# Split-f16 gate product, centred output weights and squares on ScalarE in a recurrent block with a mixture of experts

## The chip, the cores and the metric

The kernel runs on one core of one Trainium2 chip. The metric is the device time of one execution in microseconds (us). The engines are PE (TensorE), DVE (VectorE), ACT (ScalarE), POOL (GpSimd) and SP (SyncE, which here only issues DMAs). Each works through its own list of instructions in the order of the program and stops at a semaphore wait until another engine has counted it up.

## The reference

4096 tokens (16 sequences of 256) of 256 values go through two residual layers, each between layer norms. The first is the recurrent one, and it is all that the change touches:

```python
xp = layernorm(x) @ W_in.T
i, f, o, c = split(xp @ W_gate.T + b_gate)       # 4 heads x 64
i, f, o, c = exp(i), sigmoid(f), sigmoid(o), tanh(c)
cell_t = f_t * cell_{t-1} + i_t * c_t
h = o * tanh(cell * rsqrt(mean_64(cell**2) + 1e-6) * rms_w)
x = x + layernorm(h @ W_out.T)
# then x = x + layernorm(experts(layernorm(x))): router, top 4 of 16 experts, gate/up and down products
```

## The kernel before

**Stages.** First the kernel multiplies W_in into W_gate (L485), so that a block needs one gate product with a combined 256 x 1024 weight `WcT`. Then come eight blocks of 512 tokens, in ten software steps (`steps`, s = 0 to 9): step s makes the gates of block s, the cell, hidden state and output product of block s-1, and the second norm, router and routing of block s-2. POOL scatters each routed block to memory (L916, 16 indirect DMAs a block). When all are scattered, 144 tiles of 128 routed rows go through the experts (L624 to L655, L942), and the end adds and normalises (L1310 on). Every instruction's place is written by hand; there is no scheduler.

**A step on PE.** The gate product of a block has eight chunks c of 128 gate columns; each is a matmul of 512 columns for each of the two halves of the contraction (L502), into PSUM bank 2 or 3 in turn. Between them stand: after c=1 `mean_square` (L510), after c=3 the transposing and spreading of the RMS factors (L516, L525) and the transposes of block s-2 (L541), after c=4 the router (L553) and `out_product` (L533, which gives y in PSUM banks 4 and 5), before c=7 the transposes of the next block's x (L493, PSUM banks 0 and 1). In the trace each f32 matmul has two records.

**A step on ACT.** `gate_chunk` applies tanh or exp to each chunk (L723). After c=5 it also halves f (L702) and does the router's exp (L783). Weight work of the expert stage fills places (`weight_work`): squares (L792) and high halves (L804). Before chunk 7's gate `evac_x` copies the next x to `xT` (L702, two copies), once PE is through with chunk 7; behind it stand `norm_y` (L772, four instructions), `row_high` (L702) and, in the next step, `square` of the cell (L757).

**A step on DVE.** `scan` (L1010, L1016) of block s-1; `residual` of block s-2 (L1032, then statistics L1023 to L1028); `row_low` (L1118) and a weight's low half (`low`, L1211); `block_norms` (L1044 to L1055: three Newton turns on all inverse roots at once; PE's L516 waits for them); the router's tails and `slots` (L1157 to L1164, for which L553 and POOL wait); `scale_cell` (L1089), `hidden` (L1094, for which L533 waits); `choose` (L1100 to L1113); `y_stats` (L1023, on y in PSUM) and `y_norm` (L1069 to L1085, an inverse root on 128 x 4 values by Newton). The next step begins with the next `scan`, directly behind.

**At the start** DVE normalises block 0, then waits for the small weights (L989), prepares constants up to `kb_ready` (L998), for which PE's first gate product waits, and goes through the statistics of blocks 1 to 4.

The lines that decide the two orders on ACT and DVE:

```python
                    if c == CHUNKS - 1 and mid:
                        norm_y(s - 1)
...
                if mid:
                    y_stats(s - 1)
                    list(y_norm())
```

## Time and profile before

| what | value |
|---|---|
| median of 3 runs | 798.14 us (797.46 to 798.87) |
| profiled execution, its own time | 802.32 us |
| its span (first to last instruction) | 800.5 us |
| busy PE, DVE, ACT, POOL | 635.2, 537.2, 458.7, 396.1 us |
| recurrent stage (start to the last scatter) | about 0 to 369 us |
| expert tiles | about 372 to 720 us |
| end | to 800.5 us |
| granted PE clock, mean of the execution | 0.859 of 2.4 GHz |

Times in the rows are of that one execution. "x8" is a count of instructions in a row; a time in square brackets is how long the engine was idle before the row, with the engine that released it. A row's time runs from its first start to its last end, and neighbouring instructions overlap by some 0.1 us. The clock column is the share of 2.4 GHz that the chip granted TensorE; it has two levels, 1.2 and 2.4 GHz.

### The profile page before, as it was taken

The page shows a single profiled execution, that of the slowest core. Times are in us where ns is not written, and L with a number is a line of the kernel's source. Part 1 is how long each engine was busy: PE and PEld are TensorE (multiplying, and loading weights), DVE is VectorE, ACT ScalarE, POOL GpSimd, SP SyncE. Part 2 cuts the span into 40 slices and gives each one's busy share as a digit, 9 for nine tenths or more (in the row PEclk, how much of TensorE's full clock was granted, in tenths as well). Part 3 has the DMA queues.
Part 4 walks back from the last instruction along what each step waited for, and adds up shares of the span by engine and source line. Part 5 has one row for each costly group of instructions (what it writes and reads, how often), then busy time and mean ns, then how long its engine had stood idle before and what let it go on. Part 6 is the DMA issues. An engine that isn't in the chain of part 4 may idle for free.

```text
span 800.5 us, 13282 instructions
## 1 busy us (share of the span) xinstructions
PE 635.2 (79%) x3658; PEld 408.9 (51%) x3658; DVE 537.2 (67%) x1570; ACT 458.7 (57%) x933; POOL 396.1 (49%) x300
## 2 busy tenths in 40 slices
PE   5887979598998752302999999999999999997450
PEld 2344636264565541201666666666666666664230
DVE  3637487778878978500777777777777777771892
ACT  2777686547546533101666767767767767762242
POOL 0012214654845737752466666666666656565121
PEclk9979798889989856555999999999999999997555
DMA  7966754799522223253677777776777676645987
GB/s 250 423 238 106 150 92 71 224 318 347 158 86 101 89 72 119 106 207 99 112 114 110 111 113 111 108 114 109 113 113 114 108 114 102 108 58 76 350 149 102
DMA packets 111895, 115.35 MB, mean 144 GB/s; under 512 B 31730, under 2 KB 101506, under 8 KB 110162
## 3 DMA queue, kind: packets, MB, share of 16 engines
q0 software_dynamic: 35456, 50.35, 37.2%
q1 hardware_dynamic: 76370, 64.16, 26.7%
q8 instruction: 34, 0.56, 0.3%
q14 instruction: 35, 0.29, 0.1%
HBM read 55.15 MB, written 59.31 MB: 143 GB/s over the span
## 4 chain that ended last, share of the span: by engine, by line
PE 59%; DVE 12%; DMA 8%; POOL 7%; ACT 6%; issue 5%; SPq 2%; POOLq 0%; ACTq 0%; DVEq 0%
PE PS L633 8%; PE PS L634 8%; PE PS L635 8%; PE PS L502 7%; POOL routed L916 6%; PE PS L624 4%; PE PS L653 4%; PE PS L641 4%; PE PS L654 4%; PE PS L655 4%; PE PS L525 2%; PE PS L533 2%; DMA W<-w_dn 2%; DMA W<-neg_mem 1%; DVE small L1325 1%
## 5 line engine op out<-in xcount | busy, mean ns | idle before, releaser
L942 POOL DMA_INDIRECT sums<-arena x144 | 223.2, 1550 | 143.8 <-ACT arena L702 71.5
L916 POOL DMA_INDIRECT routed<-arena,small x128 | 142.7, 1115 | 90.6 <-DVE small L1162 45.3
L1303 DVE TENSOR_SCALAR arena<-PS,small 128x256 f32<-128x256 f32 x144 | 78.3, 544 | 126.7 <-ACT arena L875 124.7
L702 ACT ACTIVATE arena<-PS 128x512 f16<-128x512 f16 (+1 forms) x180 | 105.1, 589 | 78.7 <-PE PS L624 45.7
L502 PE MATMUL PS<-arena 128*128 128x512 f32 x256 | 134.0, 668 | 10.7 <-ACT arena L702 10.6
L875 ACT ACTIVATE arena<-PS,small 128x256 f32<-128x256 f32 x144 | 68.1, 473 | 104.1 <-PE PS L635 104.1
L633 PE MATMUL PS<-W,arena 128*128 x288 | 110.2, 382 | 0.0
L634 PE MATMUL PS<-W,arena 128*128 x288 | 110.1, 382 | 0.0
L635 PE MATMUL PS<-W,arena 128*128 x288 | 109.9, 382 | 0.0
L502 PEld LDWEIGHTS PS<-arena 128*128 128x128 f32 x256 | 51.9, 214 | 69.3 <-issue 65.8
L624 PE MATMUL PS<-ident,arena 128*128 128x128 f16 x576 | 56.3, 221 | 36.7 <-DMA arena<-routed 35.9
L624 PEld LDWEIGHTS PS<-ident,arena 128*128 128x128 f16 x576 | 44.4, 99 | 71.6 <-issue 39.7
L653 PE MATMUL PS<-W,arena 128*128 x288 | 78.5, 273 | 2.5 <-DVE arena L1293 2.5
L654 PE MATMUL PS<-W,arena 128*128 x288 | 78.6, 273 | 0.0
L655 PE MATMUL PS<-W,arena 128*128 x288 | 78.5, 273 | 0.0
L927 POOL DMA_DIRECT2D W<-neg_mem x16 | 19.7, 1478 | 114.5 <-ACT W L792 114.5
L723 ACT ACTIVATE arena<-PS,small 128x512 f32<-128x512 f32 x64 | 43.6, 691 | 56.3 <-PE PS L502 56.1
L1305 DVE SCALAR_TENSOR_TENSOR arena<-arena,small 128x256 f32<-128x256 f32 x144 | 69.9, 485 | 5.1
L702 ACT ACTIVATE arena<-PS,arena 128x256 f32<-128x256 f32 x144 | 69.6, 483 | 3.8 <-PE PS L655 3.7
L1293 DVE SCALAR_TENSOR_TENSOR arena<-PS,small,arena 128x256 f16<-128x256 f32 x144 | 68.8, 479 | 1.7 <-ACT arena L702 1.7
L702 ACT ACTIVATE arena<-PS,small 128x256 f16<-128x256 f32 x144 | 68.5, 476 | 0.0
L1304 DVE SCALAR_TENSOR_TENSOR arena<-arena,PS 128x256 f32<-128x256 f32 x144 | 59.2, 411 | 0.0
(164 smaller groups left out, 1023.3 us busy)
## 6 DMA issues: line engine op xcount, KB each, us to landing
arena<-routed SPq DMA_DIRECT2D x144, 128.0 KB
W<-w_gu SPq DMA_DIRECT2D x8, 1024.0 KB, 23.6
W<-neg_mem POOLq DMA_DIRECT2D x16, 512.0 KB, 8.5
sums<-zero SPq DMA_DIRECT2D x2, 4096.0 KB, 26.2
...
```

What stands on the lines that cost most here:

```text
L502: last = mm(PS[:, 2 + c % 2, :], WcT[:, k, c * P:(c + 1) * P], xT[:, k, :], start=(k == 0), stop=(k == KT - 1))
L624: last = nc.tensor.transpose(xT16[:, k * P:(k + 1) * P], xrow[j % UN][:, k * P:(k + 1) * P], ident16[:, :])
L633: mm(acc, xq[j % NX][:, k, :], hi, start=(k == 0), stop=False)
L634: mm(acc, xq[j % NX][:, k, :], lo, start=False, stop=False)
L635: last = mm(acc, xq[j % NX][:, KT + k, :], hi, start=False, stop=(k == KT - 1))
L653: mm(acc, ah[j % 2][:, k, :], hi, start=(k == 0), stop=False)
L654: mm(acc, ah[j % 2][:, k, :], lo, start=False, stop=False)
L655: last = mm(acc, al[j % 2][:, k, :], hi, start=False, stop=(k == KT - 1))
L702: return nc.scalar.activation(o, i, ACT.Copy, **kw)
L916: pool.indirect_dma_start(routed, bass.IndirectOffsetOnAxis(ap=idx, axis=0), rows[b][:, jk // TOPK, :], None).then_inc(rows_sent[lane], 16)
L942: pool.indirect_dma_start(sums[j % SUMS], bass.IndirectOffsetOnAxis(ap=dst[j % MU], axis=0), yb[u], None, compute_op=ALU.add).then_inc(y_s ...
L1303: L.send(v.tensor_scalar(up[j % 2], acc[:, FF:2 * FF], gu_hi, gu_lo, ALU.min, ALU.max))
```

## The change

Four edits, all in the recurrent stage.

- `WcT` and `xT` are held as pairs of f16 arrays, a high half and the remainder, after scaling by powers of two. A gate chunk is then three f16 products for each half of the contraction (high x high, high x low, low x high): six matmuls of 512 columns. The scale of `WcT` comes from its largest magnitude, found at the start.
- ACT's `evac_x` writes x's high half; a new DVE function `x_low` makes the low half, at the end of each DVE step, behind `y_norm`. The weight's halves are made at the start by ACT and DVE.
- The columns of W_out are centred once at the start, so that y has mean zero. Instead of DVE's statistics of y in PSUM, ACT sums its squares (`square_y`, at chunk 6), and DVE's `y_stats` waits for them.
- `norm_y` is gone. `residual` multiplies y in PSUM by its inverse root and adds it to x, in four instructions.

```diff
@@ -185,9 +185,10 @@
             return arena[0:parts, lo:lo + n]
 
 
-        WcT = cut(KT * GATES).rearrange("p (k g) -> p k g", k=KT)
+        WcT = cut(KT * GATES).bitcast(f16).rearrange("p (h k g) -> p h k g", h=2, k=KT)
         xn = cut(BT * DIM).rearrange("p (j d) -> p j d", j=BT)
-        xT = cut(KT * BLK).rearrange("p (k t) -> p k t", k=KT)
+        xT_flat = cut(KT * BLK)
+        xT = xT_flat.bitcast(f16).rearrange("p (h k t) -> p h k t", h=2, k=KT)
         g_i, g_c, g_f = [cut(PART).rearrange("p (k t) -> p k t", k=PAIRS) for _ in range(3)]
         cell = cut(PART).rearrange("p (k t) -> p k t", k=PAIRS)
         stage = at[0]
...
@@ -482,7 +484,7 @@
             for n in range(2):
                 for m in range(KT):
                     for k in range(KT):
-                        last = mm(PS[:, 2 * n + m, :], WiT[:, k, m * P:(m + 1) * P],
+                        last = mm(PS[:, 4 + 2 * n + m, :], WiT[:, k, m * P:(m + 1) * P],
                                   WgT[:, k, n * 512:(n + 1) * 512], start=(k == 0), stop=(k == KT - 1))
                     last.then_inc(wc_mm, 1)
 
...
@@ -496,11 +498,16 @@
             def gates(t, c):
                 if t or c >= 2:
                     pe.wait_ge(gate_act, 8 * t + (c - 1))
+                if c == 0:
+                    pe.wait_ge(xT_ready, KT * (t + 1))
+                    pe.wait_ge(xl_ready, KT * (t + 1))
+                if t == 0 and c % (CHUNKS // 2) == 0:
+                    pe.wait_ge(wc_low, KT * (c // (CHUNKS // 2) + 1))
                 for k in range(KT):
-                    if c == 0:
-                        pe.wait_ge(xT_ready, 2 * t + (k + 1))
-                    last = mm(PS[:, 2 + c % 2, :], WcT[:, k, c * P:(c + 1) * P], xT[:, k, :],
-                              start=(k == 0), stop=(k == KT - 1))
+                    whi, wlo = [WcT[:, h, k, c * P:(c + 1) * P] for h in range(2)]
+                    mm(PS[:, 2 + c % 2, :], whi, xT[:, 0, k, :], start=(k == 0), stop=False)
+                    mm(PS[:, 2 + c % 2, :], whi, xT[:, 1, k, :], start=False, stop=False)
+                    last = mm(PS[:, 2 + c % 2, :], wlo, xT[:, 0, k, :], start=False, stop=(k == KT - 1))
                 last.then_inc(gate_mm, 1)
 
             def mean_square(t):
...
@@ -528,6 +535,8 @@
 
             def out_product(t):
                 pe.wait_ge(h_ready, t + 1)
+                if t == 0:
+                    pe.wait_ge(wr_ready, 4)
                 for j in range(BT):
                     for q in range(PAIRS):
                         last = mm(PS[:, 4 + j // 2, (j % 2) * DIM:(j % 2 + 1) * DIM], hT[:, q, j * P:(j + 1) * P],
...
@@ -596,9 +605,10 @@
                         ranks(s - 2)
 
             pe.wait_ge(s_const, 32)
+            pe.wait_ge(peak_ready, 1)
+            nc.tensor.transpose(PS[:, 2, 0:P], spread, ident).then_inc(peak_mm, 1)
+            transposes_x(0)
             pe.wait_ge(s_w, 16 * 8)
-            pe.wait_ge(wc_copy, 4)
-            transposes_x(0)
             pe.wait_ge(kb_ready, 1)
             steps(step)
 
...
@@ -701,15 +711,10 @@
             def copy(o, i, **kw):
                 return nc.scalar.activation(o, i, ACT.Copy, **kw)
 
-            for n in range(2):
-                for m in range(KT):
-                    act.wait_ge(wc_mm, 2 * n + m + 1)
-                    copy(WcT[:, m, n * 512:(n + 1) * 512], PS[:, 2 * n + m, :]).then_inc(wc_copy, 1)
-
             def evac_x(t):
                 for k in range(KT):
                     act.wait_ge(xT_mm, 2 * t + (k + 1))
-                    copy(xT[:, k, :], PS[:, k, :]).then_inc(xT_ready, 1)
+                    copy(xT[:, 0, k, :], PS[:, k, :], scale=float(2 ** X_BITS)).then_inc(xT_ready, 1)
 
             def gate_chunk(t, c):
                 kind, q = c // 2, c % 2
...
@@ -722,7 +727,7 @@
                 act.wait_ge(gate_mm, 8 * t + (c + 1))
                 nc.scalar.activation((g_c, g_i, g_f, g_o[t % 2])[kind][:, q, :], PS[:, 2 + c % 2, :],
                                      ACT.Exp if kind == 1 else ACT.Tanh, bias=bG[:, c:c + 1],
-                                     scale=1.0 if kind < 2 else 0.5).then_inc(gate_act, 1)
+                                     scale=g_whole if kind < 2 else g_half).then_inc(gate_act, 1)
                 if c == 5:
                     act.wait_ge(gate_act, 8 * t + 6)
                     copy(g_f, g_f, bias=0.5, scale=0.5).then_inc(f_ready, 1)
...
@@ -764,14 +769,14 @@
                 act.wait_ge(cn_ready, t + 1)
                 nc.scalar.activation(cn, cn, ACT.Tanh, scale=rmsw).then_inc(tanh_ready, 1)
 
-            def norm_y(t):
-                act.wait_ge(r2_ready, t + 1)
+            def square_y(t):
+                act.wait_ge(y_mm, t + 1)
                 if t:
                     act.wait_ge(log_mm, t)
                 for j in range(BT):
                     last = nc.scalar.activation(yn[:, j, :], PS[:, 4 + j // 2, (j % 2) * DIM:(j % 2 + 1) * DIM],
-                                                ACT.Identity, bias=mr2[:, j:j + 1], scale=r2[:, j:j + 1])
-                last.then_inc(yn_ready, 1)
+                                                ACT.Square, accum_out=ysq[:, j:j + 1])
+                last.then_inc(ysq_ready, 1)
 
             def evac_x2(t):
                 for k in range(KT):
...
@@ -826,8 +831,8 @@
                         evac_x(s + 1)
                     if new:
                         gate_chunk(s, c)
-                    if c == CHUNKS - 1 and mid:
-                        norm_y(s - 1)
+                    if c == CHUNKS - 2 and mid:
+                        square_y(s - 1)
                     if c == CHUNKS - 1 and old:
                         row_high(s - 2)
                     if c == 1 and on(s, -1):
...
@@ -844,6 +849,10 @@
             act.wait_ge(r1_ready, 1)
             norm_x(0)
             evac_x(0)
+            act.wait_ge(wc_scaled, 1)
+            for n in range(2):
+                for m in range(KT):
+                    copy(WcT[:, 0, m, n * 512:(n + 1) * 512], PS[:, 4 + 2 * n + m, :], scale=wc_scale).then_inc(wc_high, 1)
             act.wait_ge(half_b, 1)
             steps(step)
 
...
@@ -986,6 +995,37 @@
             dve.wait_ge(s_x[0], 16)
             stats_x(0)
             norms_x(0, BT)
+            for i in range(2 * KT):
+                dve.wait_ge(wc_mm, i + 1)
+                last = v.tensor_reduce(wc_peak[:, i:i + 1], PS[:, 4 + i, :], AX, ALU.max, apply_absolute_value=True)
+            L(last)
+            L(v.tensor_reduce(peak, wc_peak, AX, ALU.max))
+            v.tensor_copy(spread, peak.to_broadcast([P, P])).then_inc(peak_ready, 1)
+            dve.wait_ge(peak_mm, 1)
+            L(v.tensor_reduce(peak_all, PS[:, 2, 0:P], AX, ALU.max))
+            L(v.tensor_scalar(expo, peak_all.bitcast(i32), 23, None, ALU.logical_shift_right))
+            L(v.tensor_scalar(expo, expo, EXP_LOW, None, ALU.max))
+
+            def power(o, sign, exponent):
+                return v.tensor_scalar(o.bitcast(i32), expo, sign * 2.0 ** 23, exponent * 2.0 ** 23, ALU.mult, ALU.add)
+
+            power(wc_scale, -1, 268).then_inc(wc_scaled, 1)
+            power(g_whole, 1, -14 - X_BITS)
+            power(g_half, 1, -15 - X_BITS).then_inc(wc_scaled, 1)
+            dve.wait_ge(wc_scaled, 2)
+
+            def x_low(t):
+                for k in range(KT):
+                    dve.wait_ge(xT_ready, KT * t + k + 1)
+                    v.scalar_tensor_tensor(xT[:, 1, k, :], PS[:, k, :], float(2 ** X_BITS), xT[:, 0, k, :],
+                                           ALU.mult, ALU.subtract).then_inc(xl_ready, 1)
+
+            x_low(0)
+            for i in range(2 * KT):
+                n, m = i // KT, i % KT
+                dve.wait_ge(wc_high, i + 1)
+                v.scalar_tensor_tensor(WcT[:, 1, m, n * 512:(n + 1) * 512], PS[:, 4 + i, :], wc_scale,
+                                       WcT[:, 0, m, n * 512:(n + 1) * 512], ALU.mult, ALU.subtract).then_inc(wc_low, 1)
             dve.wait_ge(s_w, 16 * 8)
             v.tensor_scalar(bG[:, 4:8], bG[:, 4:8], 0.5, None, ALU.mult).then_inc(half_b, 1)
             v.tensor_tensor(WrT[:, 0, :], WrT[:, 0, :], r_sub, ALU.subtract).then_inc(wr_ready, 1)
...
@@ -997,6 +1037,10 @@
             v.tensor_copy(ident16[:, :], ident).then_inc(ident16_ready, 1)
             v.tensor_copy(KB[:, :], KBf).then_inc(kb_ready, 1)
             L(v.tensor_copy(dest, K[:, C_DEST:C_DEST + BT]))
+            L(v.tensor_reduce(wo_mean, WoT, AX, ALU.add))
+            L(v.tensor_scalar(wo_mean, wo_mean, 1.0 / DIM, None, ALU.mult))
+            for q in range(PAIRS):
+                v.tensor_scalar(WoT[:, q, :], WoT[:, q, :], wo_mean[:, q:q + 1], None, ALU.subtract).then_inc(wr_ready, 1)
             dve.wait_ge(s_x[1], 16)
             stats_x(1)
             norms_x(BT, 2 * BT)
...
@@ -1028,8 +1072,11 @@
                 L(v.tensor_scalar(nv[:, 0:BT], mv[:, :, 1], eps, None, ALU.add))
 
             def residual(t):
-                dve.wait_ge(yn_ready, t + 1)
-                L(v.tensor_tensor(block_x(t), block_x(t), yn, ALU.add))
+                for j in range(BT):
+                    last = v.scalar_tensor_tensor(block_x(t)[:, j, :], PS[:, 4 + j // 2, (j % 2) * DIM:(j % 2 + 1) * DIM],
+                                                  r2[:, j:j + 1], block_x(t)[:, j, :], ALU.mult, ALU.add)
+                last.then_inc(res_done, 1)
+                dve.wait_ge(res_done, t + 1)
                 stats(lambda j: block_x(t)[:, j, :], mv3, LN_EPS)
 
             def block_norms(t, mid, old, ahead):
...
@@ -1060,10 +1107,10 @@
 
             def y_stats(t):
 
-                dve.wait_ge(y_mm, t + 1)
-                stats(lambda j: PS[:, 4 + j // 2, (j % 2) * DIM:(j % 2 + 1) * DIM], mv2, 4 * LN_EPS)
-
-            def y_norm(done=r2_ready):
+                dve.wait_ge(ysq_ready, t + 1)
+                L(v.tensor_scalar(nv[:, 0:BT], ysq, 1.0 / DIM, 4 * LN_EPS, ALU.mult, ALU.add))
+
+            def y_norm():
 
                 a, b, y, x = na[:, 0:BT], nb_[:, 0:BT], ny[:, 0:BT], nv[:, 0:BT]
                 n = L.send(v.tensor_scalar(a.bitcast(i32), x.bitcast(i32), 1, None, ALU.logical_shift_right))
...
@@ -1082,7 +1129,6 @@
                     n = L.send(v.scalar_tensor_tensor(r2 if turn == 2 else y, b, 1.5, y, ALU.add, ALU.mult))
                 yield
                 L.wait(n)
-                v.scalar_tensor_tensor(mr2, mv2[:, :, 0], -1.0, r2, ALU.mult, ALU.mult).then_inc(done, 1)
 
             def scale_cell(t):
                 dve.wait_ge(rb_mm, t + 1)
...
@@ -1257,6 +1300,8 @@
                     list(y_norm())
                 if s == 3:
                     peak_row(0)
+                if on(s, -1):
+                    x_low(s + 1)
                 if s == 8:
                     low()
                 if s == NBLK + 1:
```

ACT, around the output product of step 5 (L723, now L728, are the gates' activations; L804, now L809, a weight's high half; L702 x2, now L712 x2, are `evac_x`; L772 `norm_y`; L777 `square_y`). Before:

```order
L723 ACTIVATE arena<-PS,small 128x512
L702 ACTIVATE arena<-arena 128x1024
L783 ACTIVATE small<-small 128x16
L723 ACTIVATE arena<-PS,small 128x512
L804 ACTIVATE W<-W,small 128x1024
L702 ACTIVATE arena<-PS 128x512 x2
L723 ACTIVATE arena<-PS,small 128x512
L772 ACTIVATE arena<-PS,small 128x256 x4
L702 ACTIVATE arena<-x_own 128x4x256
L757 ACTIVATE arena<-arena 128x1024
```

The same place in the changed kernel:

```order
L728 ACTIVATE arena<-PS,small 128x512
L712 ACTIVATE arena<-arena 128x1024
L788 ACTIVATE small<-small 128x16
L728 ACTIVATE arena<-PS,small 128x512
L777 ACTIVATE arena,small<-PS 128x256 x4
L809 ACTIVATE W<-W,small 128x1024
L712 ACTIVATE arena<-PS 128x512 x2
L728 ACTIVATE arena<-PS,small 128x512
L712 ACTIVATE arena<-x_own 128x4x256
L762 ACTIVATE arena<-arena 128x1024
```

The four instructions on y have moved ahead of the weight's high half and of `evac_x`, and none stands between `evac_x` and the cell's square.

DVE, end of step 4 and beginning of step 5, before (L1023 to L1028 are `y_stats`, L1069 to L1085 `y_norm`, of which the Newton turns are left out; then `scan` and `residual`):

```order
L1023 BN_STATS small<-PS 128x6 x4
L1026 BN_AGGR small<-small 128x2 x4
L1028 TENSOR_SCALAR small<-small 128x4
L1069 TENSOR_SCALAR small<-small 128x4
...
L1085 SCALAR_TENSOR_TENSOR small<-small 128x4
L1010 TENSOR_TENSOR arena<-arena 128x1024
L1016 SCALAR_TENSOR_TENSOR arena<-arena 128x256 x4
L1032 TENSOR_TENSOR X<-X,arena 128x1024
```

The same place in the changed kernel (L1111 `y_stats`, L1116 on `y_norm`, L1020 `x_low`, L1054 and L1060 `scan`, L1076 `residual`):

```order
L1111 TENSOR_SCALAR small<-small 128x4
L1116 TENSOR_SCALAR small<-small 128x4
...
L1020 SCALAR_TENSOR_TENSOR arena<-PS,arena 128x512 x2
L1054 TENSOR_TENSOR arena<-arena 128x1024
L1060 SCALAR_TENSOR_TENSOR arena<-arena 128x256 x4
L1076 SCALAR_TENSOR_TENSOR X<-PS,small,X 128x256 x4
```

The statistics are one instruction on 128 x 4 values; two instructions of `x_low` stand ahead of the scan, and the residual is four instructions instead of one.

DVE at the start, changed kernel, between block 0's norm and the constants (L1000 to L1010 find the weight's scale, L1020 is `x_low` of block 0, L1027 the weight's low halves; before, L990, now L1030, followed the norm directly):

```order
L991 SCALAR_TENSOR_TENSOR small<-small 128x4
L1000 TENSOR_REDUCE small<-PS 128x1 x4
L1002 TENSOR_REDUCE small<-small 128x1
L1003 COPY prod<-small 128x128
L1005 TENSOR_REDUCE small<-PS 128x1
L1006 TENSOR_SCALAR small<-small 128x1
L1007 TENSOR_SCALAR small<-small 128x1
L1010 TENSOR_SCALAR small<-small 128x1 x3
L1020 SCALAR_TENSOR_TENSOR arena<-PS,arena 128x512 x2
L1027 SCALAR_TENSOR_TENSOR arena<-PS,small,arena 128x512 x4
L1030 TENSOR_SCALAR small<-small 128x4
```

These 15 instructions now stand ahead of the constants (L1038 among them, which frees PE's first gate product) and of the statistics of blocks 1 to 4.

## Rows read from the trace of the kernel before

**Rows 1.** The chain that ended last, 205 to 246 us: shares by line, and one piece.

```profile
by line: PE PS L502 43.5%; PE PS L533 8.7%; ACT arena L772 6.8%; PE PS L510 6.4%; PE PS L525 5.9%; ACT arena L702 5.3%; PE PS L541 4.6%; PE PS L493 4.5%; issue 4.3%; PE PS L553 4.1%; ACT arena L723 3.1%; ACT arena L757 2.3%; ACT small L702 
...
236.90 3.43 PE PS L502 x8
```

**Rows 2.** Timeline of PE: start us, us, instruction, count, idle before it and its releaser.

```profile
94.97 3.70 PE L533 MATMUL PS<-arena 128*128 128x256 f32 x16
...
118.99 0.28 PE L516 MATMUL PS<-K,small 128*16 128x128 f32 x1 [3.17 <-DVE small L965]
...
129.24 3.70 PE L533 MATMUL PS<-arena 128*128 128x256 f32 x16
...
168.22 3.70 PE L533 MATMUL PS<-arena 128*128 128x256 f32 x16
...
192.24 0.28 PE L516 MATMUL PS<-K,small 128*16 128x128 f32 x1 [1.47 <-DVE small L965]
...
200.12 3.70 PE L533 MATMUL PS<-arena 128*128 128x256 f32 x16
...
224.16 0.27 PE L516 MATMUL PS<-K,small 128*16 128x128 f32 x1
...
233.20 3.70 PE L533 MATMUL PS<-arena 128*128 128x256 f32 x16
...
255.58 0.27 PE L516 MATMUL PS<-K,small 128*16 128x128 f32 x1
...
263.10 3.70 PE L533 MATMUL PS<-arena 128*128 128x256 f32 x16
```

**Rows 3.** Timeline of ACT behind an output product.

```profile
176.04 1.14 ACT L804 ACTIVATE W<-W,small 128x1024 f16<-128x1024 f32 x1
178.16 1.09 ACT L702 ACTIVATE arena<-PS 128x512 f32<-128x512 f32 x2 [0.99 <-PE PS L502]
...
179.70 1.94 ACT L772 ACTIVATE arena<-PS,small 128x256 f32<-128x256 f32 x4
```

**Rows 4.** Timeline of DVE in the same stretch, and one row of step 6.

```profile
174.35 0.23 DVE L1028 TENSOR_SCALAR small<-small 128x4 f32<-128x4 f32 x1
...
176.90 1.22 DVE L1010 TENSOR_TENSOR arena<-arena 128x1024 f32<-128x1024 f32 x1
...
181.67 1.23 DVE L1032 TENSOR_TENSOR X<-X,arena 128x1024 f32<-128x1024 f32 x1 [0.97 <-ACT arena L772]
...
222.00 0.17 DVE L1055 SCALAR_TENSOR_TENSOR small<-small 128x4 f32<-128x4 f32 x1
```

**Rows 5.** Timeline of ACT, 31 to 34 us: the squares of a weight slab.

```profile
31.82 1.06 ACT L792 ACTIVATE W<-W 128x1024 bf16<-128x1024 f32 x1 [0.72 <-DMA W<-w_dn]
32.78 0.19 ACT L792 ACTIVATION_READ_ACCUMULATOR W<-W 128x1 f32 x1
```

**Rows 6.** Page, part 5: a VectorE subtraction of halves over 256 columns.

```profile
L1293 DVE SCALAR_TENSOR_TENSOR arena<-PS,small,arena 128x256 f16<-128x256 f32 x144 | 68.8, 479 | 1.7 <-ACT arena L702 1.7
```

**Rows 7.** The same operation over 1024 columns: duration ns min/median/max.

```profile
L1211 DVE SCALAR_TENSOR_TENSOR W<-W,small x24: 1272/1282/1285, 60.6 to 308.7; 128x1024 f16<-128x1024 f32 x24
```

**Rows 8.** The chain at 500 us: one f16 product of 512 columns.

```profile
500.89 0.22 PE PS L633
```

**Rows 9.** Timeline of ACT, DVE and PE at the start.

```profile
16.27 0.60 ACT L702 ACTIVATE arena<-PS 128x512 f32<-128x512 f32 x1 [1.12 <-PE PS L485]
...
17.49 0.27 DVE L998 CAST KB<-W 128x256 bf16<-128x256 f32 x1
...
20.84 1.67 PE L502 MATMUL PS<-arena 128*128 128x512 f32 x2
```

**Rows 10.** Timeline of DVE: its wait for block 6 of x.

```profile
153.25 1.41 DVE L973 BATCH_NORM_STATS2 small<-X 128x6 f32<-128x256 f32 x4 [2.90 <-DMA X<-x]
```

**Rows 11.** Timeline of POOL: first scatter behind its last wait for VectorE.

```profile
295.41 0.97 POOL L916 DMA_INDIRECT routed<-arena,small  x1 [10.59 <-DVE small L1162]
```

**Rows 12.** One stretch: length; PE, PEld, DVE, ACT, POOL busy; clock; DMA share; GB/s.

```profile
116.00:130.00 14.00, 10.66 (x49) 8.10 (x50) 10.25 (x39) 7.44 (x14) 0.22 (x1) 0.76 0.01 1
```

27 lines of the change are left out of this document (13 added, 14 removed).

## The prediction, made before the changed kernel ran

> **What bounds the kernel now.** I read the busy tenths first: PE is nearly full through the expert tiles, which the change doesn't touch, so all the difference must arise before 372 us. Then the end of that stage, on POOL: its last wait for DVE ended at 295.41, after 10.6 us of idling [rows 11]. From there POOL scatters block 5, 6 and 7 without another wait for an engine; whatever DVE's slots of block 5 gain or lose, the kernel gains or loses, one for one (a gain up to the 10.6 us a block that POOL idles there, and in the blocks ahead likewise).
>
> Then the chain within a step: of 205 to 246 us the gate product L502 has 43.5%, the norm of y on ACT (L772) 6.8% [rows 1]. That speaks for the change. But a chain only names who came last. The timelines show how near the others are. I measure a step from the end of L533, when y is ready: 98.67, 132.94, 171.92, 203.82, 236.90 and 266.80 us for steps 2 to 7 (start plus length, [rows 2]), so some 30 to 39 us a step. In steps 3 and 5 PE stands idle ahead of L516 (3.17 and 1.47 us), released by DVE's `block_norms`; in steps 6 and 7 it doesn't, PE being later than DVE [rows 2]. In step 6 the last of DVE's norms ends at 222.17, 18.3 us behind y, and PE starts L516 at 224.16, 20.3 us behind it [rows 2, 4]. DVE has 2 us of slack there, and none in steps 3 and 5. So the question is what the change does to DVE's list.
>
> **What the change removes from PE.** Two chunks of the f32 product, eight records, take 3.43 us [rows 1], 1.72 a chunk. An f16 product of 512 columns takes 0.22 [rows 8], so six of them 1.3 us; in the low clock it is 3.4 and 2.6. That is 0.43 us a chunk, 3.4 a block, 27 over the stage, if PE were the only bound.
>
> **What it does to the path behind y.** Step 5, y ready at 171.92. Before: ACT is through the activations of chunks 5 and 6 at 176.04 (+4.1), and `evac_x` starts at 178.16 (+6.2), when PE has ended chunk 7 [rows 3]. Meanwhile DVE makes the statistics of y; the inverse root runs from 174.35 to 176.90, and the scan starts at 176.90, 4.98 behind y [rows 4]. Nothing here waits for ACT.
>
> After, the same list:
> - chunk 5 is ready 0.43 earlier, so ACT is through chunk 6's activation at +3.7.
> - `square_y`: four activations with an accumulator. The four of `norm_y` took 1.94 [rows 3]; each accumulation adds a read of 0.19 [rows 5]: 2.7 us, so y's sums are there at +6.4. DVE, which has nothing else in its list here, waits for them: this is the new wait.
> - the inverse root as before, 2.55 [rows 4]: +8.9.
> - `x_low`, two instructions of 512 columns. No such row exists; the same operation takes 0.479 us on 256 columns with a PSUM source [rows 6] and 1.28 on 1024 [rows 7], so the two lie between 1.0 and 2.6 together. I take the straight line, 0.75 each: +10.4. They don't wait for ACT: the high half of the weight (1.05) and `evac_x` end near +8.6.
> - scan at +10.4 instead of +4.98: 5.4 later.
> - `residual`: it no longer waits for `norm_y` (0.97 of idling gone), but is four instructions of about 0.45 instead of one of 1.23 [rows 4, 6]. Before it ended at 182.90 (+10.98). After: scan's 3.8 us to +14.2, then 1.8: +16.0.
>
> So everything behind it on DVE, the block norms with it, stands **5.0 us later** against y. By the Trainium skill ("VectorE: DVE Perf Modes", The TRN2 errata) a VectorE instruction with a PSUM source costs 120 cycles and one per element at 0.96 GHz, an estimate of 0.66 us for 512 columns. By that the 5.0 would be 4.8. No run here shows it.
>
> On ACT the wait for `norm_y` is gone, but the cell's square now waits for the scan (+14.2). PE's first gate chunks of the block need `x_low` and start at +10.4; before, one copy of `evac_x` behind +6.2 was enough. PE is through with chunk 7 some 1.3 us (three chunks at 0.43) sooner, at +4.9, and idle until then. Two chunks (2.6 to 5.2), the mean squares (some 2 us, not before +15.2), two chunks more: +19.8 to +24. DVE's norms end at 18.3 + 5.0 = +23.3 in a step like 6. PE has become the waiting one in the high clock.
>
> **The sum, step by step**, each as its lengthening:
> - Step 3: L516 was DVE's already, at +20.3 [rows 2]. ACT has a weight's square (1.2) between the chunks there, so `square_y` comes later still and the shift is 6.1. Behind L516 PE was in the low clock, and one chunk there gives 0.9 back: 5.2.
> - Step 4: the residual did not wait for `norm_y` there before, so less is given back: shift 5.7. But DVE waits 2.90 for block 6 of x there [rows 10], a DMA chain that begins with squares of step 3 and moves with them. It hides 2.9: 2.8, and 0.5 back on a chunk: 2.3.
> - Step 5: 5.0, and the clock. In step 3 an idle stretch of 3.17 ahead of L516 went with a clock of 0.76 of full from 116 to 130 us [rows 12], and L516 to the next y took 13.95 against 11.58 in step 5 [rows 2]. Here PE will idle some 5 us ahead of the chunks and 3 ahead of L516. 13.95 less the chunk's 0.9 is 13.1: 1.5 more, 6.5.
> - Step 6: L516 from +20.3 to +23.3, 12.74 behind it becomes 13.1: 3.3.
> - Step 7: L516 from +18.7 to +23.1, 11.22 becomes 13.1: 6.3.
> - Step 8: no `x_low` (scan 4.0 later), the residual 0.6 longer and without a wait before: 4.6, down to the slots of block 5.
> - Step 2: PE-bound at L516 like step 6: 3.
>
> That is 31. **The start:** DVE now has 15 instructions ahead of the constants. The last piece of the combined weight is there at 16.27 us, when ACT copied it before [rows 9]. One reduction of 512 columns (0.7) and the chain for the scale, nine small ones of some 0.2 with a transpose between, end near 18.9; `x_low`, which waits for ACT's high halves, near 20.9; four low halves of 0.75: 23.9; then the constants, seven small ones, 1.1 us, of which the last ended at 17.76 before [rows 9]: 25.0. PE's first gate product, at 20.84 before [rows 9], waits for that: 4 us. Step 0 is a chain of gates and ACT's squares behind it and has nothing to hide it. The centring (some 1.5 us) delays the norm of block 1, in parallel. I take 4, bounds 3 and 7.
>
> The sum is **35 us**: span 800.5 to 835.5, the profiled run's own time 802.3 to 837. The median of the runs is 4.2 below the profiled time, so the prediction is 798.1 + 35 = **833**. Its own range: `x_low` at its two bounds (-0.5 and +1.1 a step over six steps: -3, +7), the clock's share (nothing or double: -5, +5), the start (-1, +3): 820 to 848.
>
> **The rivals.**
> - *PE is the bound and stays it, faster.* For it: L502's share of the chain [rows 1]. If ACT's sums cost DVE nothing, steps 2, 6 and 7 could gain the 2.0 us by which PE is behind DVE at L516, and every step 0.4 on the chunk behind it: 9 us, 789. Against it: `square_y` stands behind three activations and a half-scaling of f, all of them behind y; it decides only if the sums come within 1 us of y. 6%.
> - *The shift is partly swallowed.* The slack of DVE at L516 (2.0 in step 6) may be more elsewhere in a step, and `square_y` cheaper than `norm_y` with reads. If half of each step's lengthening goes: +17, 815. 15%.
> - *The clock stays low.* With pauses of 3 to 5 us twice a step PE could run most of it at 1.2 GHz. Then L533 takes twice its 3.7 us [rows 2]; that alone is 3.4 a step over what I have, in six steps: +20, 853. The stretch of [rows 12] shows the clock at 0.76 around one pause. The Trainium skill has such a rule ("TensorE: Matmul & The Clock Gate", HAM oscillation): bursts that are shorter than the waits between them run in the low clock again and again. By that rule the time is this rival's; the stretch at 116 us, with one pause, agrees as far as it goes. 15%.
> - *No change.* What PE gains (27 us at most) would have to meet what DVE loses (31) within 2 us, or the squares be fetched in PE's shadow at no cost: 798. 3%.
>
> My forecast has the remaining 61%. A measurement of this kernel tells about 0.2% from no change. Faster: 6%; within 0.2%: 3%; slower: 91%. The range leaves out the faster case and the far end of the clock's: 812 to 850.
>
> **What the changed profile would show.** DVE's `y_stats` (L1111) idle some 5 to 6 us each step, released by ACT L777; `scan` some 10.4 us behind the end of L533 instead of 5.0; `x_low` at 0.75 us; PE idle ahead of the first gate chunk, for DVE, about 5 us; L516 released by DVE in every step; the first gate product at 25 us; POOL's first scatter of block 5 near 330; the expert stage as long as before. The prediction is wrong if the gap between y's product and the scan stays near 5 us, or if PE's stretch from L516 to y becomes shorter than 11.6 us by more than the chunk's 0.4.

## The result, and the profile after

The changed kernel takes **836.39 us** (median of 4 runs, 831.06 to 840.96) against 798.5 for the kernel before on the same chip (4 runs, 797.46 to 801.88): ratio 1.046, 95% interval 1.039 to 1.054. Its profiled execution took 831.06 us, the fastest of the four, with a span of 829.3. It is slower by 28.8 us of span, or 38 us between the medians; the prediction was 833. Single executions can be disturbed (one of early_x_start, below, took 915.63 us at a clock of 0.683): medians and ranges count them, ratios leave them out.

Some matmul records are missing from the traces; where I give the end of an output product, it is the end of its full row.

First PE's timeline of the changed kernel, steps 4 to 7, the same rows as [rows 2]. L523 is now the transpose of the RMS factors (L516 before), L542 the output product (L533 before).

```profile
170.01 0.38 PE L523 MATMUL PS<-K,small 128*16 128x128 f32 x1 [7.49 <-DVE small L974]
...
180.15 3.70 PE L542 MATMUL PS<-arena 128*128 128x256 f32 x16
...
207.69 0.38 PE L523 MATMUL PS<-K,small 128*16 128x128 f32 x1 [4.79 <-DVE small L974]
...
217.77 3.70 PE L542 MATMUL PS<-arena 128*128 128x256 f32 x16
...
243.11 0.38 PE L523 MATMUL PS<-K,small 128*16 128x128 f32 x1 [2.64 <-DVE small L974]
...
255.15 6.10 PE L542 MATMUL PS<-arena 128*128 128x256 f32 x16
```

From step 2 on L523 is released by DVE in every step, also in steps 2, 6 and 7, where L516 waited for nobody before. Between these rows a step has two halves: from y (end of L542) to L523, and from L523 to the next y. In step 5 the first is 23.84 us (20.32 before), the second 13.78 (11.58 before, from [rows 2]).

Next DVE's timeline of step 5, with y ready at 183.85; it answers to [rows 4].

```profile
189.31 0.17 DVE L1111 TENSOR_SCALAR small<-small 128x4 f32<-128x4 f32 x1 [4.78 <-ACT arena L777]
...
191.80 1.29 DVE L1020 SCALAR_TENSOR_TENSOR arena<-PS,arena 128x512 f16<-128x512 f32 x2
193.01 1.21 DVE L1054 TENSOR_TENSOR arena<-arena 128x1024 f32<-128x1024 f32 x1
194.36 2.44 DVE L1060 TENSOR_TENSOR_SCAN arena<-arena 128x256 f32<-128x256 f32 x4
196.72 1.63 DVE L1076 SCALAR_TENSOR_TENSOR X<-PS,small,X 128x256 f32<-128x256 f32 x4
```

DVE stands idle for 4.78 us, until ACT has summed the squares, 5.5 us behind y. The scan starts 9.2 us behind y (4.98 before), the residual ends at +14.5 (10.98 before): 3.5 us later, which is the first half's lengthening to the tenth.

ACT's timeline of the same place shows why the sums come no sooner; it answers to [rows 3].

```profile
185.18 0.78 ACT L728 ACTIVATE arena<-PS,small 128x512 f32<-128x512 f32 x1 [4.72 <-PE PS L510]
185.99 1.06 ACT L712 ACTIVATE arena<-arena 128x1024 f32<-128x1024 f32 x1
186.96 0.20 ACT L788 ACTIVATE small<-small 128x16 f32<-128x16 f32 x1
187.06 0.76 ACT L728 ACTIVATE arena<-PS,small 128x512 f32<-128x512 f32 x1
187.73 0.37 ACT L777 ACTIVATE arena<-PS 128x256 f32<-128x256 f32 x1
187.99 0.19 ACT L777 ACTIVATION_READ_ACCUMULATOR arena<-PS 128x1 f32 x1
...
190.19 1.10 ACT L712 ACTIVATE arena<-PS 128x512 f16<-128x512 f32 x2
```

Two gate activations, the halving of f and an exp of the router stand ahead of the squares. The squares themselves take 1.55 us together (187.73 to 189.28, the last read's end), since each one's read of the accumulator overlaps the next.

The waits of the stage, 40 to 372 us (engine, line, released by; us in total, times, longest):

```profile
DVE small L1111 <- ACT arena L777: 45.3, 8, 11.7
...
PE PS L508 <- DVE arena L1020: 37.2, 7, 6.7
...
PE PS L523 <- DVE small L974: 27.7, 7, 7.5
```

These are the new waits: 45 us of DVE for ACT, and 65 us of PE, which waits for `x_low` ahead of its first gate chunk and for the block norms ahead of L523. In the kernel before PE waited 27 us in these two places (10.6 for `evac_x`, 16.2 at L516). Last POOL, as in [rows 11]: its first scatter of block 5, 32.8 us later than before.

```profile
328.16 0.97 POOL L925 DMA_INDIRECT routed<-arena,small  x1 [16.58 <-DVE small L1208]
```

Of the 32.8 us the two scatters behind give 2.4 back (POOL waited for DMAs there before): the first expert product starts at 403.95 instead of 373.57, and the rest is 1.6 us shorter than it was.

**Where the 32.8 us are.** I added up the two halves over all steps from the rows of L523 and of the output product, for both kernels and for the experiments below (one profiled execution each):

| profiled execution of | first L523 | y to L523, steps 2 to 8 | L523 to y, steps 1 to 7 | L523 to the slots of block 5, step 8 | first scatter of block 5 |
|---|---|---|---|---|---|
| before | 52.5 | 143.0 | 88.5 | 11.5 | 295.4 |
| changed | 56.1 | 162.3 | 98.5 | 11.3 | 328.2 |
| warm | 56.6 | 162.5 | 91.5 | 11.3 | 321.9 |
| start_first | 58.1 | 162.1 | 104.5 | 11.3 | 335.9 |
| early_x_start | 54.5 | 134.0 | 96.3 | 11.3 | 296.2 |
| early_f32 | 52.6 | 135.9 | 83.5 | 11.3 | 283.3 |
| early_x_pad | 58.9 | 137.2 | 96.6 | 11.3 | 304.0 |
| early_x_warm | 54.5 | 138.3 | 91.5 | 11.3 | 295.6 |
| y_squares | 51.6 | 158.2 | 90.0 | 11.3 | 311.1 |
| y_psum | 53.2 | 136.1 | 96.1 | 11.3 | 296.6 |
| f16_y_psum | 57.7 | 146.9 | 92.9 | 11.3 | 308.8 |
| scan_first | 57.6 | 167.3 | 95.3 | 11.3 | 331.5 |
| sq_early | 56.1 | 144.7 | 104.2 | 11.3 | 316.4 |
| sq_early_scan_first | 56.1 | 136.8 | 95.4 | 11.3 | 299.6 |

The change costs 19.3 us in the first half (DVE's list), 10.0 in the second, 3.6 ahead of the first L523. In the second half PE goes through the same f32 work as before, but more of it in the low clock. The groups of PE's instructions, 40 to 260 us (busy us, mean ns of one), before:

```profile
L533 PE MATMUL PS<-arena 128*128 128x256 f32 x96 | 22.3, 385 | 0.6 <-DVE arena L1094 0.6
L525 PE MATMUL PS<-small,K 16*128 16x128 f32 x112 | 17.3, 313 | 4.3 <-ACT small L702 4.3
```

and in the changed kernel:

```profile
L542 PE MATMUL PS<-arena 128*128 128x256 f32 x92 | 26.2, 448 | 1.1 <-DVE arena L1140 1.1
L532 PE MATMUL PS<-small,K 16*128 16x128 f32 x96 | 19.9, 386 | 2.9 <-ACT small L712 2.9
```

One record of the output product takes 448 ns instead of 385, one of the spreading 386 instead of 313. Records overlap, so I price them by busy time: 0.285 us a record instead of 0.232, and 0.207 instead of 0.154; 16 of each make 1.7 us a step. The windows say the same of the clock (length, then PE, PEld, DVE, ACT, POOL busy, the granted clock, DMA share, GB/s); before:

```profile
180.00:220.00 40.00, 34.72 (x143) 20.95 (x143) 34.96 (x114) 27.06 (x45) 24.15 (x21) 0.91 0.80 253
```

Changed:

```profile
180.00:220.00 40.00, 30.41 (x147) 20.57 (x147) 29.96 (x109) 21.47 (x38) 18.79 (x19) 0.79 1.00 320
```

PE is busy 4.3 us less in 40 and gets 0.79 of full speed instead of 0.91; from 220 to 260 us it is 0.70 instead of 0.87.

### The profile page after: what moved, and what is told of

The parts are those of the page before. It is cut to its first block, busy times and chain, and to the rows that moved or that the text cites. A ratio compares the mean times of both kernels' runs of the same rounds, so it can differ in the third digit from the quotient of the medians.

```text
span 829.3 us, 13554 instructions
## 1 busy us (share of the span) xinstructions
PE 628.6 (76%) x3787; PEld 411.4 (50%) x3787; DVE 543.0 (65%) x1558; ACT 462.2 (56%) x965; POOL 386.1 (47%) x300
## 4 chain that ended last, share of the span: by engine, by line
PE 58%; DVE 22%; ACT 6%; issue 5%; POOL 4%; DMA 3%; SPq 0%; POOLq 0%; ACTq 0%; DVEq 0%
PE PS L643 8%; PE PS L645 8%; PE PS L644 8%; PE PS L542 4%; PE PS L634 4%; PE PS L663 4%; PE PS L651 4%; PE PS L664 4%; PE PS L665 4%; POOL routed L925 4%; PE PS L532 3%; DVE arena L1060 2%; PE PS L562 2%; PE PS L550 2%; DVE X L1076 2%
## 5 line engine op out<-in xcount | busy, mean ns | idle before, releaser
L951 POOL DMA_INDIRECT sums<-arena x144 | 222.0, 1542 | 143.0 <-DMA sums<-arena 79.4
L925 POOL DMA_INDIRECT routed<-arena,small x128 | 133.8, 1045 | 119.2 <-DVE small L1208 77.7
L712 ACT ACTIVATE arena<-PS 128x512 f16<-128x512 f16 (+2 forms) x176 | 103.0, 591 | 68.9 <-PE PS L634 44.0
L508 PE MATMUL PS<-arena 128*128 128x512 f16 x128 | 59.9, 468 | 44.7 <-DVE arena L1020 37.2
L728 ACT ACTIVATE arena<-PS,small 128x512 f32<-128x512 f32 x64 | 49.2, 774 | 48.7 <-PE PS L510 48.7
L712 ACT ACTIVATE arena<-PS,arena 128x256 f32<-128x256 f32 x144 | 69.7, 484 | 3.8 <-PE PS L665 3.7
L712 ACT ACTIVATE arena<-PS,small 128x256 f16<-128x256 f32 (+1 forms) x148 | 71.0, 482 | 0.0
L509 PE MATMUL PS<-arena 128*128 128x512 f16 x128 | 58.8, 459 | 0.0
```

The lines of the kernel that those rows point to most:

```text
L712: return nc.scalar.activation(o, i, ACT.Copy, **kw)
L925: pool.indirect_dma_start(routed, bass.IndirectOffsetOnAxis(ap=idx, axis=0), rows[b][:, jk // TOPK, :], None).then_inc(rows_sent[lane], 16)
L951: pool.indirect_dma_start(sums[j % SUMS], bass.IndirectOffsetOnAxis(ap=dst[j % MU], axis=0), yb[u], None, compute_op=ALU.add).then_inc(y_s ...
```

## The experiments

Twelve kernels, in three groups; each group has its own runs of the kernel before (medians 801.0, 799.26 and 797.52 us), so I compare by ratios. A cost in us that stands behind a difference of ratios is that difference of some 800 us.

| kernel | median us (range, runs) | ratio to before, 95% |
|---|---|---|
| y_squares | 816.25 (813.93 to 821.74, 4) | 1.0185 (1.0094 to 1.0276) |
| y_psum | 798.78 (795.8 to 804.43, 10) | 0.997 (0.9931 to 1.0009) |
| f16_y_psum | 816.73 (809.24 to 830.67, 10) | 1.0146 (1.0093 to 1.0199) |
| sq_early_scan_first | 808.76 (799.36 to 811.37, 10) | 1.0064 (1.0017 to 1.0111) |
| scan_first | 836.67 (835.18 to 841.75, 4) | 1.049 (1.0426 to 1.0555) |
| warm | 831.61 (823.4 to 834.83, 4) | 1.0425 (1.0365 to 1.0484) |
| start_first | 838.3 (833.98 to 841.09, 6) | 1.0488 (1.044 to 1.0537) |
| early_x_start | 810.49 (802.4 to 915.63, 6) | 1.0148 (1.0095 to 1.0202) |
| sq_early | 820.84 (812.12 to 825.51, 4) | 1.0217 (1.0164 to 1.027) |
| early_f32 | 791.58 (785.25 to 804.95, 7) | 0.99 (0.9858 to 0.9943) |
| early_x_pad | 804.51 (800.92 to 811.32, 8) | 1.0094 (1.0054 to 1.0135) |
| early_x_warm | 804.16 (800.12 to 805.88, 6) | 1.0074 (1.0045 to 1.0104) |

**The theory and its rivals.** Theory: the 35 us come from DVE's list, on which the wait for ACT's sums and `x_low` now stand between y and the scan. Rival one: they come from the f16 product and the low clock. Rival two: the start.

### The change in halves: y_squares, y_psum, f16_y_psum

y_squares is the kernel before with all of the change but the f16 product. y_psum is that with y's statistics on DVE as before, so ACT has neither `norm_y` nor squares. f16_y_psum is the changed kernel with the statistics on DVE. The edit that y_psum and y_squares share:

```diff
-                dve.wait_ge(yn_ready, t + 1)
-                L(v.tensor_tensor(block_x(t), block_x(t), yn, ALU.add))
+                for j in range(BT):
+                    last = v.scalar_tensor_tensor(block_x(t)[:, j, :], PS[:, 4 + j // 2, (j % 2) * DIM:(j % 2 + 1) * DIM],
+                                                  r2[:, j:j + 1], block_x(t)[:, j, :], ALU.mult, ALU.add)
```

> The kernel before with the y half of the change alone: centred output weights, squares of y on ScalarE behind chunk 6, residual from PSUM; the gate product stays f32 and there is no x_low. If VectorE's wait for the squares is the main cost: the sums come 6.8 us behind y, the scan starts at about 9.3 us behind y instead of 5.0, the residual's stretch is 4 us later, five to seven steps of it, so 798 + 20 = 818 us (812 to 824). If the f16 gate product and the clock it leads to are the main cost: within 3 us of before, 795 to 801.

> The kernel before with centred output weights and the residual from PSUM, but y's statistics on VectorE as before; no squares on ScalarE, and the four instructions of norm_y gone. The list theory: VectorE's order is as before, its wait of 0.97 us for norm_y goes and 0.4 us of residual comes, ScalarE has 1.8 us less ahead of the cell's square, so steps 6 and 7 gain up to 2 us and the others 0.6 to 1: 790 us (786 to 795). If reading y from PSUM four times is itself what costs: 800 or more.

> The changed kernel without the squares on ScalarE: y's statistics on VectorE again (y_stats reads PSUM), all else as changed. The list theory: x_low waits for evac_x, which PE now frees at 4.9 us behind y, so the scan starts near 6.9 us behind y instead of 10.4; with the start's 3 us and the pause of PE that is left: 806 us (800 to 812). If the f16 product with its low clock is the main cost: 825 or more.

By the ratios the squares on ACT cost 2.2% with f32 gates (1.0185 to 0.997) and 3.1% with f16 gates (1.0464 to 1.0146), some 17 and 25 us; the f16 product, with its `x_low` and its longer start, costs 1.8% or 2.7%, 14 or 22 us. Whether the two together cost more than their sum is within these intervals. y_squares at 816 is what the list theory gave; f16_y_psum, 812 by its ratio, lies at the upper edge of that theory's range and far from the 825 of the other.

This pair alone does not price the clock, since f16_y_psum has `x_low` and the start in it too. The table separates them. The squares lengthen the first half by 22 us (y_psum to y_squares), which is DVE's wait. The f16 product on top of y_psum makes the first L523 4.5 us later and the first half 10.8 longer, by the start and by `x_low`, and the second half 3.2 shorter: no cost of a low clock is to be seen there. Only where the squares are present too (y_squares to changed) does the second half grow, by 8.5 of the 17.1 us at the scatter. So the list holds the largest part (19.3 of the 32.8 us at the scatter) and the start (rival two) 3.6; rival one shows in one of the two pairs only.

y_psum missed its 790, and the table says where. The first half is 6.9 us shorter than in the kernel before, so the list did get shorter; the second is 7.6 longer, with the same f32 instructions. The windows of that half in step 5, the kernel before and then y_psum:

```profile
192.20:203.80 11.60, 10.55 (x62) 8.52 (x63) 10.41 (x38) 6.08 (x10) 4.04 (x5) 1.00 1.06 317
191.50:206.30 14.80, 14.44 (x62) 11.68 (x63) 10.55 (x38) 6.18 (x10) 5.97 (x6) 0.69 0.97 290
```

The granted clock is 0.69 instead of 1.00, behind a wait of PE for the block norms of 4.04 us instead of 1.47. Over 40 to 300 us that wait is

```profile
PE PS L517 <- DVE small L957: 24.1, 6, 8.2
```

and was 16.2 us in the kernel before (L516), four times. PE reached the transpose earlier, waited longer there, and went through more of what follows in the low clock. In this execution the clock took back what the list gave; the ratio, 0.997, says that on average nothing measurable is left. It also shows that a low clock in the second half doesn't need the f16 product.

### The order on DVE and ACT: sq_early_scan_first, scan_first, sq_early

On the changed kernel, the squares ahead of chunk 5's activation, and `x_low` behind the scan:

```diff
+                    if c == 5 and mid:
+                        square_y(s - 1)
                     if new:
                         gate_chunk(s, c)
-                    if c == CHUNKS - 2 and mid:
-                        square_y(s - 1)
...
                 if mid:
                     scan(s - 1)
+                    if s < NBLK - 0 and s >= 2:
+                        x_low(s)
...
-                if on(s, -1):
-                    x_low(s + 1)
+                if s == 0:
+                    x_low(1)
```

> The changed kernel with square_y ahead of chunk 5's activation instead of behind chunk 6's, and x_low behind the next step's scan instead of ahead of it. No work is added or removed. The list theory: sums 2.7 us behind y, scan at 5.3 instead of 10.4, x_low ends at 10.4 as now, the residual ends at 12 instead of 16: 4 us a step less, 836 - 25 = 811 us (804 to 818). If the clock after PE's pause is what costs (the pause ahead of the first gate chunk stays as it is): 830 or more.

> The changed kernel with one edit: in a step, x_low stands behind the scan instead of ahead of it. DVE's list as the cause: the scan and all behind it come 1.2 us earlier in each of six steps, and what x_low sometimes waits for evac_x is hidden too; 836 becomes about 822 (815 to 828), though PE's first gate chunk starts some 3.8 us later. Clock and PE as the cause: the longer pause ahead of the gate chunk costs more than the scan gains, 834 or more.

> The changed kernel with one edit: square_y stands ahead of the activation of chunk 5, so that y's sums are there some 3 us behind y instead of 5.5. scan_first alone gave nothing and both together gave 28 us. If DVE's wait for the sums is what the squares cost: 812 (806 to 820). Rival, that the two edits need each other: 828 or more.

Both edits together give back 4.0% of the 4.6%: some 32 us by the ratios come back without one instruction less. The squares' place alone gives 2.5% (20 us; 816 by the ratio, inside its 806 to 820, the median 820.84 just outside): DVE's wait for the sums in step 5 falls from 4.78 to 0.96 us. The place of `x_low` alone gives nothing, against my expectation, and 1.5% (12 us) once the squares are early.

DVE's timeline of scan_first in step 5 (y at 184.40) says why:

```profile
192.39 1.22 DVE L1054 TENSOR_TENSOR arena<-arena 128x1024 f32<-128x1024 f32 x1
...
196.11 1.26 DVE L1020 SCALAR_TENSOR_TENSOR arena<-PS,arena 128x512 f16<-128x512 f32 x2
197.29 1.65 DVE L1076 SCALAR_TENSOR_TENSOR X<-PS,small,X 128x256 f32<-128x256 f32 x4
```

The scan starts 8.0 us behind y instead of 9.2. But `x_low` has only moved from ahead of the scan to behind it and still stands ahead of the residual, which ends 14.5 us behind y as it did; the block norms, and L523 at +23.9, come no sooner. My expectation that "the scan and all behind it" gain 1.2 us overlooked that. The price is PE's: its first gate chunk starts 13.1 us behind y instead of 9.4, and it gets to L523 only 1.0 us ahead of DVE; in step 4 DVE waits 3.12 us for a transpose behind PE's late first chunk, and that step's first half is 2.9 us longer.

With early squares there is a wait that the scan can fill. In sq_early DVE waits for `evac_x` ahead of `x_low`, 13.0 us in six steps, which it does not do between 60 and 300 us of the changed kernel. In step 5:

```profile
189.21 1.29 DVE L1020 SCALAR_TENSOR_TENSOR arena<-PS,arena 128x512 f16<-128x512 f32 x2 [1.67 <-ACT arena L712]
```

With the scan in this gap (sq_early_scan_first) L523 stands 20.1 us behind y instead of 21.7, and the first half is 7.9 us shorter over the steps. The second half is 8.8 shorter between these two executions as well; how much of that the edit brings is open, since that half varies by itself (see start_first).

### The clock: warm

On the changed kernel, 14 dummy matmuls in PE's pause for `x_low`, with a result that nobody reads:

```diff
+                if c == 0 and t >= 2:
+                    for _ in range(14):
+                        mm(PS[:, 6, 256:512], WcT[:, 0, 0, 0:P], WcT[:, 0, 0, 0:256], start=True, stop=True)
                 if c == 0:
                     pe.wait_ge(xT_ready, KT * (t + 1))
```

> The changed kernel with 14 extra f16 matmuls of 256 columns ahead of the first gate chunk of blocks 2 to 7, written to a place in PSUM that nobody reads, so that PE is not idle in the pause for x_low. They end before x_low does. DVE's list as the cause: 831 to 838, the low clock in the gate chunks costs next to nothing because PE then waits for DVE anyway. Low clock as a cause of a good part of the 35 us: 821 to 828, with the granted clock of the stretch 0 to 370 us clearly above 0.73.

The median, 831.6, lies at the edge of the list theory's range; the interval of its ratio overlaps that of the changed kernel. Its profiled execution, 823.4, is the fastest of its four, so I use it only for the place: in the table above the first half of the steps is unchanged (162.5 against 162.3), the second is 7.0 us shorter. So the dummies touched the second half only. By the ratios a gain is not established.

### The start: start_first

```diff
+            dve.wait_ge(s_const, 32)
+            v.tensor_copy(KB[:, :], KBf).then_inc(kb_ready, 1)
             dve.wait_ge(peak_mm, 1)
```

and the halving of the bias behind two of the four low halves of the weight.

> The changed kernel with one edit at the start: the cast of KB stands behind the peak's broadcast and the bias's halving behind two of the weight's four low halves, so that PE's first gate product waits for x_low and two low halves only. The first product should start at some 21.8 us instead of 23.6. If the start's delay goes through to the end as the prediction has it: 834 (832.5 to 835). Rival: step 1 has a wait of 11.7 us for the squares of y that takes up the difference, 836 to 837.

838.3: nothing gained. The first gate product did start at 22.46 instead of 23.63, though the whole start (the transpose of the peak, 18.23 for 17.03) was 1.2 us later in this execution. The expectation's ranges, 832.5 to 835 and 836 to 837, both missed it. ACT's timeline shows another wait behind it, for DVE's norm of block 1:

```profile
31.04 2.07 ACT L738 ACTIVATE arena<-X,small 128x256 f32<-128x256 f32 x4 [3.33 <-DVE small L991]
```

In the changed kernel this wait is 0.74 us:

```profile
30.04 2.08 ACT L738 ACTIVATE arena<-X,small 128x256 f32<-128x256 f32 x4 [0.74 <-DVE small L991]
```

So once the first product is earlier, the norm of block 1 holds ACT. It stands behind all 18 new instructions and the centring on DVE, and moving the constants leaves it where it is (31.01 and 30.01 us, of which 1.2 is this execution's later start). That this is all that start_first lost is not shown. The table shows something else of use: the first half of the steps repeats to within 0.2 us between these two executions (162.3 and 162.1), and the second differs by 6 us (98.5 and 104.5), with the same instructions. So the scatter of such a kernel's times can come from there.

### x off the path, and the f16 product by itself: early_x_start, early_f32

Two `xT` buffers (the second in the place of `yn`; the transposed second norm goes into the row buffers), PE's transposes of the next x behind chunk 3, where PE and ACT wait for `block_norms`, `evac_x` beside them, `x_low` behind `block_norms`, statistics on DVE:

```diff
+                    if c == 3 and on(s, -1):
+                        transposes_x(s + 1)
                     if c == 3 and mid:
                         rms_transpose(s - 1)
...
                 if mid or old:
                     block_norms(s - 1, mid, old, ahead)
+                if on(s, -1):
+                    x_low(s + 1)
```

early_x_start has the start of start_first too. early_f32 has the same order with the f32 product, and so no `x_low`.

> The changed kernel with four edits: statistics of y on DVE again (no squares on ACT); two xT buffers, so that PE's transposes of the next x stand behind gate chunk 3, evac_x beside them and x_low behind block_norms, all off the path from y to the scan; the transposed second norm goes to the row buffers to make room; the start as in start_first. DVE's list as the cause: x_low's 17 us (816 against 799) go, and the start's 2 as well, and PE keeps what f16 gives it: 787 (775 to 797), faster than the kernel before. Rival, that the f16 product costs by itself (more instructions, lower clock): 808 or more.

> The kernel before with statistics on DVE and the residual from PSUM as in y_psum, f32 gates, and two xT buffers, with the x transposes behind chunk 3 and evac_x beside them: the twin of early_x_start without the f16 product. If the f16 product costs by itself (low clock in the f32 products around it): 790 (784 to 797), some 20 us less than early_x_start's 810. Rival, that the early transposes are what costs in early_x_start: 805 or more.

early_x_start came out at 810, not at 787: my expectation that PE keeps what f16 gives it was wrong. By the ratios it is not even faster than f16_y_psum (1.0146), though its first half is 12.9 us shorter in the profiled executions; its own, 802.4, is the fastest of its runs and 8 us below their median. early_f32, its twin, takes 1.0% less than the kernel before, the fastest kernel of this study; f16 costs 2.5% against it (some 20 us). In the table the twins have the same first half (134.0 and 135.9 us, so `x_low` is hidden from it) and differ by 12.8 in the second, which is all of the 12.9 by which the scatter of block 5 is later (2.0 at the start less 1.9 in the first half aside); another 4.3 us between their profiled executions arise behind it, and I have not traced them. PE's timeline of step 5 in early_x_start, from the spreading to the output product:

```profile
189.57 3.04 PE L534 MATMUL PS<-small,K 16*128 16x128 f32 x16 [0.36 <-ACT small L716]
192.55 1.97 PE L552 MATMUL PS<-K,x_own 128*128 128x128 f32 x8
...
196.87 2.04 PE L564 MATMUL PS<-arena 128*128 128x16 f32 x16
198.76 3.70 PE L544 MATMUL PS<-arena 128*128 128x256 f32 x16
```

and in early_f32:

```profile
183.73 2.05 PE L529 MATMUL PS<-small,K 16*128 16x128 f32 x16 [0.71 <-ACT small L710]
185.78 1.06 PE L547 MATMUL PS<-K,x_own 128*128 128x128 f32 x8
186.69 1.88 PE L506 MATMUL PS<-arena 128*128 128x512 f32 x4
188.81 1.96 PE L559 MATMUL PS<-arena 128*128 128x16 f32 x16 [0.24 <-DVE small L1167]
190.62 3.70 PE L539 MATMUL PS<-arena 128*128 128x256 f32 x16
```

The same f32 work takes 3.04 and 1.97 us instead of 2.05 and 1.06, and the gate chunk between (194.31 to 196.87) 2.56 in f16 at the low clock against 1.88 in f32 mostly at the high one. A part of the 12.8 is not the clock: by the groups of 40 to 260 us PE waited 4.1 us for DVE's slots ahead of the router's product in early_x_start and 0.2 in early_f32, since `x_low` stands ahead of the slots. And y_psum, with f32 gates, has a second half as long as that of early_x_start (96.1 and 96.3): what the twins show is the price of the f16 product in this order, and not that it brings the low clock by itself.

### Filling PE: early_x_pad, early_x_warm

early_x_pad repeats a product twice ahead of each chunk, which the chunk overwrites; early_x_warm has 14 dummy matmuls behind chunk 3.

```diff
+                if t:
+                    for _ in range(2):
+                        mm(PS[:, 2 + c % 2, :], WcT[:, 0, 0, c * P:(c + 1) * P], xT[t % 2][:, 0, 0, :], start=True, stop=True)
                 for k in range(KT):
...
+                    if c == 3 and old and new:
+                        pe.wait_ge(gate_act, 8 * s + 3)
+                        for _ in range(14):
+                            mm(PS[:, 2, 0:256], WcT[:, 0, 0, 0:P], WcT[:, 0, 0, 0:256], start=True, stop=True)
```

> early_x_start with two more f16 products of 512 columns ahead of each gate chunk from block 1 on, overwritten by the chunk itself: eight instead of six, so that PE has as much to do per chunk as with f32. If PE's spare time is what lowers the clock, and the low clock is the cost: not slower than 810, with a granted clock over 0.831, perhaps 800. If PE's work is what counts: 820 or more. If f16 products themselves bring the low clock: clock below 0.83 and 820 or more.

> early_x_start with 14 extra f16 matmuls of 256 columns behind chunk 3 of blocks 2 to 7, in PE's wait for block_norms. If the pause there costs the clock of the products from rms_spread to out_product: 800 (795 to 805). Rival: the clock falls whatever is done in the pause, 810 to 818.

A third more of f16 work on PE (112 products, 25 us at 0.22) makes the kernel no slower: 1.0094 against 1.0148, the intervals overlapping. All its eight executions had a granted clock of 0.851 to 0.862, the five behind early_x_start's ratio 0.823 to 0.841. That is the first reading of my expectation: PE's spare time goes with the low clock, and filling it pays for itself. So f16's shorter gate time is worth nothing that shows in this kernel; whether more work is free because PE had slack, or because the clock rose with it, this run doesn't tell.

The dummies in the pause give 1.0074, intervals just overlapping as well: it looks like a gain of 6 us, which these runs don't establish; in the table the second half is 4.8 us shorter and the first 4.3 longer. Neither comes near early_f32's 0.99. What of the 20 us between the f16 and the f32 twin is the clock, and what `x_low` and the start, is settled only as far as the profile rows above go.

## Why the prediction was right, and where it was off

The sign and the size came out (833 against 836.4, inside 820 to 848), and so did the mechanism: a new wait of DVE for ACT, `x_low` ahead of the scan, L523 released by DVE from step 2 on, slots of block 5 later by what the stage loses. The terms were less good than the sum, and that it came within 3.4 us of the median is partly luck: 9.6 us too much in the first half, 7.7 too little in the second, 4.0 that came back behind the scatter and had no term, and a profiled execution that took 831, 6 us less than the 837 forecast for it. The range has a slip too: its own bounds (-3, -5, -1) add up to 824, not 820.

- **The new wait.** Predicted at y + 6.4 in step 5, measured +5.5. The squares with their reads were put at 2.7 us and took 1.55. I added the reads to the activations, but they overlap, as [rows 5] already shows (the read starts 0.96 us behind the start of an activation of 1.06); and a square took 0.38 us where one of `norm_y` had taken 0.58.
- **`x_low`.** Put at 0.75 each between bounds of 0.5 and 1.3; the scan starts 1.21 behind the first, 0.60 each. The VectorE page of the Trainium skill ("VectorE: DVE Perf Modes", The TRN2 errata) gives an estimate of 0.66 us for it; the start's four low halves, from 19.71 to 22.34, agree with that, one starting every 0.66 us (0.74 each by itself), and `x_low` with one every 0.60 (0.68 each) is a little cheaper.
- **Scan and residual.** Scan at +9.2 for 10.4, the residual's end at +14.5 for +16.0, a shift of 3.5 instead of 5.0. Every step's first half was predicted 1.1 to 1.7 us too long (step 5: 25.3, measured 23.84; step 6: 23.3, measured 21.64). Over steps 2 to 8 the list cost 19.3 us; by the prediction's terms without the clock's and the chunk's share it was 29.
- **Step 4** gained its hidden wait as said: DVE's 2.90 for block 6 of x [rows 10] is gone, and the first half grew by 1.5 only.
- **The second half** was the term that was too small. Per step I had L523 to y at 13.1 us from step 5 on; it measured 13.78, 18.14 and 13.50. Together with the 3.3 more of step 1, in which the output product took 6.16 us in the low clock and which I had not costed at all, the half grew by 10.0 where I had some 2.3. Step 2's was 2.5 shorter, which I had not forecast either. The rival "the clock stays low" had a true mechanism, at some 8 of the 20 us I gave it. Whether the errors in both halves cancel depends on the execution: the second half is what varies. The rule of the Trainium skill that I had weighed ("TensorE: Matmul & The Clock Gate", HAM oscillation) is about bursts shorter than the waits between them. Here the bursts were the longer ones: in step 5 waits of 4.45 and 4.79 us had 9.7 us of products between them. Behind each wait the products ran in the low clock, and each time the high one came back (at 200.15 and near 215.6 us), so the clock in the window of step 5 was 0.79 instead of 0.91 and not at the low level for good.
- **The start.** The gate product came 2.8 us later for 4 predicted, the first L523 3.6 later. The working counted 15 new instructions on DVE; they are 18. The sentence that the centring "delays the norm of block 1, in parallel" was wrong: ACT waits for this norm, 0.74 us here and 3.33 in start_first.
- **"PE is the bound, faster"** fell by f16_y_psum, early_x_start and early_x_pad: with y's sums on DVE the f16 kernel is still 1.5% slower than the kernel before, with `x_low` off the path as well it is no better, and though the gate product had 43.5% of the chain [rows 1], a third more of f16 work on top of it costs nothing that shows.

What I had wrong in kind is what the f16 product is worth. The prediction costed only what it adds around itself and gave it 0.4 us a chunk behind L523. Even with `x_low` out of the way (early_x_start) it loses to its f32 twin.
